# Causal attention: row maxima of two heads in one VectorE instruction over two PSUM banks

## The chip, the cores and the metric

The kernel runs on one core of one Trainium2 chip. The metric is the device time of one execution in microseconds (us). The engines named below are TensorE (PE, with its weight loads as PEld), VectorE (DVE), ScalarE (ACT), GpSimd (POOL) and SyncE (SP), which only issues DMAs. A PSUM bank holds 512 f32 numbers for each of 128 partitions.

## The reference, cut to what matters

The kernel computes one whole layer: a norm, a compressed, selected and windowed attention, a second norm, causal attention with 16 query and 4 key heads, and a mixture of 8 experts. The change touches the causal attention alone (here B = 2 batches, S = 2048 tokens, 16 numbers a head):

```python
q = _apply_rope(q, cos, sin)
k = _apply_rope(k, cos, sin)
scores = jnp.einsum('bqhd,bkhd->bhqk', q, k) * scale
causal = jnp.tril(jnp.ones((S, S), dtype=bool))
scores = jnp.where(causal[None, None], scores, jnp.finfo(scores.dtype).min)
probs = jax.nn.softmax(scores, axis=-1)
attn = jnp.einsum('bhqk,bkhd->bqhd', probs, v).reshape(B, S, NH * HD)
```

The softmax needs the largest score of each row before its exponentials can be taken.

## The kernel before, in words

`stage6` does this attention, about half of the span. Its work goes by 8 groups `gi` (2 batches x 4 key heads), each with `GRP` = 4 query heads, and in a group by 4 chunks `c` of 512 queries. Every score is computed twice.

**The main steps.** `STEPS` lists 320 steps (gi, c, kt), 40 in a group, where kt is a tile of 128 keys. For a step, TensorE multiplies keys by queries for 4 heads into `pS` (line 1558; I call one of these an S), with a second small matmul that adds the mask where the tile lies on the diagonal (line 1562). The matmul takes the row maximum with it, as three extra rows of `QT`. ScalarE takes the exponential into `prob` (line 1674, 3 slots of `pS`), and TensorE multiplies `prob` by the values into `pO` (line 1577: 4 heads, called PV). PV of step n - 1 stands in the middle of step n, and S of step n + 1 is issued in step n. When a chunk of queries is through, VectorE copies `pO` to `oS` (line 1747, `chunk`), and the first PV of the next chunk waits for that copy (`o_out`). TensorE then transposes `oS` into a bank of `pM` (line 1586, item O), and VectorE divides out of it (lines 1754 and 1756).

**The row maxima.** Ahead of that, a "unit" U (gi, head, query tile qt, part of 512 keys) computes the scores of 128 queries against up to 512 keys into one of `BANKS` = 4 banks of `pM` (line 1542), and VectorE takes the maximum of each row. Off the diagonal (part < qt // 4; 96 of the 160 units of a group) that is `reduce_max` over one full bank (line 1731). On the diagonal (64 units of 128 to 512 columns) it is an instruction that adds `mask_row` and takes the maximum (line 1727), with a short one that reads the result. After the last unit of a chunk one small VectorE instruction joins the parts (line 1739, `mneg`), POOL splits the result in three, and an item M transposes it into a bank (line 1533), from which ScalarE copies it to `mrow` and SP puts it into `QT`.

**What sets the order.** `background` lists units and M items; `schedule` gives every step its share of them by `cost`; in a step TensorE issues them at five places (`some(0)` to `some(4)`): ahead of the first S, after the first S, after the second S, after PV, and after the third S. `Plan` hands out the banks of `pM` in that order, one after the other, to U, M and O alike, and notes for each what must have left its bank before (`clear`). TensorE takes its instructions in order, so a unit that waits for its bank holds back the S and PV behind it. VectorE takes the units in the same order, and the copy of `pO` stands behind the units of its step. The units of chunks 0 and 1 of the first group, and some more, come ahead of the first step (`before`).

Of the kernel before, what the change touches and what calls it, by code (L numbers as in the profile page):

```python
# [30 lines left out]
P = 128  # L31
# [1126 lines left out]
def background():  # L1158

    items = []  # L1160
    for gi in range(NG):
        for c in range(CH):
            items += [("U", gi, h, qt, part) for h in range(GRP) for qt in range(4 * c, 4 * c + 4) for part in range(c + 1)]
            items.append(("M", CH * gi + c))

    for k in range(CH * NG - 1):
        at = items.index(("M", k))
        items.insert(at + 10, items.pop(at))
    return items
# [55 lines left out]
class Plan:  # L1225


    def __init__(self):
# [12 lines left out]
        for n, item in enumerate(order):  # L1241
            by = {"M": "mrow_out", "U": "unit_max", "O": "o_put"}[item[0]]
            counts[by] += 1
            self.bank[item], self.clear[item], self.count[item] = n % BANKS, last[n % BANKS], counts[by]
            last[n % BANKS] = (by, counts[by])
        self.units_through = {}
        for k in range(CH * NG):
            self.units_through[k] = max(self.count[x] for x in order if x[0] == "U" and CH * x[1] + x[3] // 4 == k)
        self.last_unit = {x: CH * x[1] + x[3] // 4 for x in order
                          if x[0] == "U" and self.count[x] == self.units_through[CH * x[1] + x[3] // 4]}  # L1250


def stage6(nc, sb, ps, sem, env, base_env):
# [7 lines left out]
    with ExitStack() as ctx:  # L1261
# [81 lines left out]
        with nc.Block() as block:  # L1343
# [150 lines left out]
            def _(pe):  # L1494
# [22 lines left out]
                    project(i)  # L1517

                def take(item):
                    if plan.clear[item] is not None:  # L1520
                        name, count = plan.clear[item]
                        pe.wait_ge(s[name], count)
                    return plan.bank[item]

                def beside(item):
# [162 lines left out]
            def _(dve):  # L1688
# [25 lines left out]
                assert first.k == 15  # L1714

                def beside(item):
                    if item[0] != "U":
# [4 lines left out]
                    if part == qt // 4:  # L1722
                        if plan.count[item] <= 2:
                            dve.wait_ge(s.masks, 1)
                        else:
                            dve.wait_ge(s.unit_max, plan.count[item] - 2)
                        nc.vector.tensor_tensor_reduce(junk[:, plan.count[item] % 2, 0:w], pM[:, plan.bank[item], 0:w],  # L1727
                                                       mask_row[:, 512 - w:512], 1.0, -3e38, ALU.add, ALU.max,
                                                       mx[:, h, qt, part:part + 1]).then_inc(s.unit_max, 1)
                    else:  # L1730
                        nc.vector.reduce_max(mx[:, h, qt, part:part + 1], pM[:, plan.bank[item], 0:w],  # L1731
                                             AX.X).then_inc(s.unit_max, 1)
# [816 lines left out]
```

## Time and profile before

| | |
|---|---|
| time, median of 3 runs | 1742.45 us (1739.26 to 1745.59) |
| span of the profiled execution | 1739.7 us |
| TensorE busy in it | 1630.1 us (94%) |
| VectorE busy | 1173.3 us (67%) |
| ScalarE busy | 946.3 us (54%) |
| granted TensorE clock, mean | 0.966 |
| the steps of the causal attention | about 352 to 1221 us |
| one group of 40 steps | 108.4 us |

The span is the time from the first to the last instruction of one profiled execution on the core; the profile has no other time of that execution, so the 2.75 us between the span and the median are taken as what lies around it. Busy time counts an instruction from its start to its end. Since the matmuls are pipelined, the busy time of TensorE contains the time in which a matmul drains while the next one already runs; the distance between two starts says more than the duration. A granted clock of 1.00 is 2.4 GHz and one of 0.50 is 1.2 GHz.

### The profile page before, as it was taken

The numbers are of one execution on the slowest core, as the hardware profiler recorded it, in microseconds if no ns is written. First come the engines' busy times: TensorE is split into PE (matmuls) and PEld (weight loads), VectorE is DVE, ScalarE is ACT, GpSimd is POOL, SyncE is SP. The second block draws the span as 40 slices with busy tenths as digits, with TensorE's granted clock in tenths as the row PEclk, the third lists the DMA queues.
The fourth block names the chain that finished last, engine by engine and source line by source line (L and its number), as shares of the span: only waits on it lengthen the run. The fifth ranks groups of instructions, "written<-read, shape, count | busy, mean of one in ns | idle before, by whom it ended". The sixth has DMA issues, their size and how long they took to land. (4 is left out here: it accounts for less than half of the span.)

```text
span 1739.7 us, 29572 instructions
## 1 busy us (share of the span) xinstructions
PE 1630.1 (94%) x9040; PEld 804.0 (46%) x9040; DVE 1173.3 (67%) x3195; ACT 946.3 (54%) x2069; POOL 556.3 (32%) x842
## 2 busy tenths in 40 slices
PE   7799998899999999999999999998895899999996
PEld 3367665333333333333333333332784455555564
DVE  6632788799888888888888888880685334434342
ACT  6034554256677676776767767677574233333332
POOL 3441238073515003030030300000277344444443
PEclk9899998799999999999999999999996899999999
DMA  5000000311030300303003030000378677777774
GB/s 164 0 7 19 1 2 7 61 26 38 1 62 2 59 4 1 62 2 59 5 1 62 2 61 3 2 1 1 99 238 286 117 130 129 130 129 129 132 125 71
DMA packets 252194, 105.76 MB, mean 61 GB/s; under 512 B 208064, under 2 KB 247880, under 8 KB 252040
## 3 DMA queue, kind: packets, MB, share of 16 engines
q1 hardware_dynamic: 233296, 80.62, 21.8%
q0 software_dynamic: 13392, 18.49, 6.3%
q10 hardware_dynamic: 5352, 4.76, 0.8%
q8 instruction: 76, 1.25, 0.3%
q14 instruction: 78, 0.64, 0.1%
HBM read 30.88 MB, written 23.67 MB: 31 GB/s over the span
## 5 line engine op out<-in xcount | busy, mean ns | idle before, releaser
L1674 ACT ACTIVATE prob<-pS 128x512 f32<-128x512 f32 (+3 forms) x1280 | 597.1, 534 | 256.3 <-PE pS L1562 134.1
L1731 DVE TENSOR_REDUCE mx<-pM 128x1 f32<-128x512 f32 x768 | 503.1, 686 | 70.3 <-PE pM L1542 66.5
L1542 PE MATMUL pM<-KT,QT 96*128 96x512 bf16 (+3 forms) x1280 | 444.1, 357 | 8.7 <-DMA QT<-Qt 4.6
L1558 PE MATMUL pS<-QT,KT 99*128 99x512 bf16 (+3 forms) x1280 | 416.5, 350 | 3.7 <-ACT prob L1674 2.8
L1577 PE MATMUL pO<-prob,VV 128*32 128x512 f32 (+3 forms) x2560 | 299.9, 540 | 14.6 <-ACT prob L1674 14.3
L2437 PE MATMUL bank<-w13T,QKV 128*128 x568 | 257.8, 598 | 16.5 <-ACT QKV L2464 16.5
L1727 DVE CUSTOM_DVE_ANT_0 junk<-pM,mask_row 128x128 bf16<-128x128 f32 (+3 forms) x512 | 241.6, 484 | 46.3 <-PE pM L1542 42.9
L1542 PEld LDWEIGHTS pM<-KT,QT 96*128 96x128 bf16 x1280 | 124.2, 98 | 268.5 <-DVE mx L1731 109.9
L1467 POOL CAST mpart<-mneg 128x16 bf16<-128x16 f32 x32 | 6.8, 211 | 663.2 <-DVE mneg L1739 663.2
L2497 DVE TENSOR_TENSOR QKV<-QKV,bank 128x512 f32<-128x512 f32 x71 | 48.9, 688 | 234.3 <-issue 199.1
L1558 PEld LDWEIGHTS pS<-QT,KT 99*128 99x128 bf16 x1280 | 123.6, 98 | 143.0 <-ACT prob L1674 79.8
L2418 POOL DMA_INDIRECT out_dram<-QKV x71 | 111.8, 1575 | 199.0 <-ACT QKV L2479 120.2
L2437 PEld LDWEIGHTS bank<-w13T,QKV 128*128 128x128 f32 x568 | 109.1, 192 | 124.6 <-issue 121.2
L2479 ACT ACTIVATE QKV<-bank,QKV 128x256 f32<-128x256 f32 x71 | 33.6, 474 | 206.9 <-DMA out_dram<-QKV 150.7
L2448 PE MATMUL bank<-w2T,QKV 128*128 x568 | 134.4, 380 | 2.4 <-DVE QKV L2511 2.4
L2448 PEld LDWEIGHTS bank<-w2T,QKV 128*128 128x128 f32 x568 | 108.0, 190 | 46.9 <-issue 36.0
L1562 PE MATMUL pS<-mask_kq,identb 128*128 128x128 bf16 x512 | 112.0, 221 | 0.0
L1577 PEld LDWEIGHTS pO<-prob,VV 128*32 128x32 f32 x2560 | 51.3, 108 | 114.2 <-ACT prob L1674 95.2
L2406 POOL COPY QKV<-QKV 128x512 uint16<-128x512 uint16 x71 | 81.8, 1152 | 18.0 <-issue 10.6
L1907 POOL DMA_INDIRECT queue<-QKV x64 | 65.2, 1019 | 20.9 <-issue 17.3
L1562 PEld LDWEIGHTS pS<-mask_kq,identb 128*128 128x128 bf16 x512 | 50.5, 99 | 37.3
L2464 ACT COPY QKV<-QKV 128x512 uint16<-128x512 uint16 x71 | 53.5, 754 | 20.5 <-DMA QKV<-QKV 18.5
(356 smaller groups left out, 1954.6 us busy)
## 6 DMA issues: line engine op xcount, KB each, us to landing
raw<-in_ffn_w_dram SPq DMA_DIRECT2D x48, 256.0 KB, 3.6
QKV<-queue SPq DMA_DIRECT2D x71, 136.0 KB, 2.6
out_dram<-x ACTq DMA_DIRECT2D x8, 512.0 KB, 4.7
x<-_attn_hidden_states_dram SPq DMA_DIRECT2D x14, 256.0 KB, 5.9
QKV<-QKV SPq DMA_TRANSPOSE x142, 3.3
QT<-mrow SPq DMA_DIRECT2D x128, 3.0 KB
out_dram<-QKV POOLq DMA_INDIRECT x71, 3.9
wc_s<-in_attn_Wc_dram SPq DMA_DIRECT2D x1, 1024.0 KB, 7.9
```

The costliest lines, as they stand in the source:

```text
L1542: last = nc.tensor.matmul(pM[:, bank, 0:w], QT[0:ROWS, par, h, qt * P:(qt + 1) * P], KT[0:ROWS, par, 512 * part:512 * part + w], start=Tru ...
L1558: last = nc.tensor.matmul(pS[:, p % NSC, lo:512], KT[0:ROWS + 3, par, kt * P:(kt + 1) * P], QT[0:ROWS + 3, par, h, 512 * c + lo:512 * c + ...
L1562: last = nc.tensor.matmul(pS[:, p % NSC, lo:lo + P], identb[:, :], mask_kq[:, :], start=False, stop=True)
L1577: last = nc.tensor.matmul(pO[32 * h:32 * h + 32, lo:512], VV[:, gi % 2, kt, :], prob[:, n % 3, h, lo:512], start=(kt == 0), stop=(kt == 4 ...
L1674: nc.scalar.activation(prob[:, n % 3, h, lo:512], pS[:, p % NSC, lo:512], ACT.Exp, scale=SCALE).then_inc(s.head_exp, 1)
L1727: nc.vector.tensor_tensor_reduce(junk[:, plan.count[item] % 2, 0:w], pM[:, plan.bank[item], 0:w], mask_row[:, 512 - w:512], 1.0, -3e38, AL ...
L1731: nc.vector.reduce_max(mx[:, h, qt, part:part + 1], pM[:, plan.bank[item], 0:w], AX.X).then_inc(s.unit_max, 1)
L1907: nc.gpsimd.indirect_dma_start(out=v.queue[:, :], out_offset=bass.IndirectOffsetOnAxis(ap=slots[:, t, a:a + 1], axis=0), in_=QKV[:, t, 0:R ...
L2406: nc.gpsimd.tensor_copy(xp[:, j % 2, :].rearrange("p (a n) -> p a n", a=2), apart(xq[:, j % R, 0:H], C)).then_inc(s.x_parts, 1)
L2418: nc.gpsimd.indirect_dma_start(out=v.out_rows[:, :], out_offset=bass.IndirectOffsetOnAxis(ap=tail[:, j % RT, E:E + 1], axis=0), in_=y[:, j ...
L2437: last = nc.tensor.matmul(pH[:, j % 2, a, :], xqT[:, j % 2, c * P:(c + 1) * P], w13T[:, c, bass.ds(e * (2 * FFN) + a * FFN, FFN)], start=( ...
L2448: last = nc.tensor.matmul(pY[:, j % 2, 0:H], gT[:, j % 2, f * P:(f + 1) * P], w2T[:, f, bass.ds(e * H, H)], start=(f == 0), stop=(f == FC ...
```

## The change

Off the diagonal, units of two neighbouring heads (2 pr and 2 pr + 1) with the same query tile and part become one item V. TensorE still does the two matmuls, one right after the other, now into two neighbouring banks (0 and 1, or 2 and 3), with one semaphore increment after the second. VectorE takes both rows of maxima with one `tensor_reduce` over 2 x 512 numbers. Diagonal units stay single. A V takes banks only from an even one on, so a bank is passed over where the count stands at an odd one. The order of the units is new (by pairs of heads instead of by head), M items are put 7 items later instead of 10, and `cost` gives a V 1134 where two units had 1244.

```diff
@@ background
-            items += [("U", gi, h, qt, part) for h in range(GRP) for qt in range(4 * c, 4 * c + 4) for part in range(c + 1)]
+            for pr in range(GRP // 2):
+                for qt in range(4 * c, 4 * c + 4):
+                    items += [("V", gi, pr, qt, part) for part in range(c)]
+                    items += [("U", gi, 2 * pr + n, qt, c) for n in range(2)]
...
-        items.insert(at + 10, items.pop(at))
+        items.insert(at + 7, items.pop(at))
@@ cost
+    if item[0] == "V":
+        return 2 * 512 + 110
@@ Plan
+            wide = 2 if item[0] == "V" else 1
+            if wide == 2 and free % 2:
+                free += 1
+            bank = free % BANKS
+            free += wide
...
+            before = [x for x in last[bank:bank + wide] if x]
+            self.clear[item] = [(name, max(k for n, k in before if n == name)) for name in sorted({n for n, _ in before})]
+            last[bank:bank + wide] = [(by, counts[by])] * wide
@@ stage6, TensorE
+                    if kind == "V":
+                        for n in range(2):
+                            last = nc.tensor.matmul(pM[:, bank + n, :], QT[0:ROWS, par, 2 * h + n, qt * P:(qt + 1) * P],
+                                                    KT[0:ROWS, par, 512 * part:512 * part + 512], start=True, stop=True)
+                        last.then_inc(s.unit_mm, 1)
+                        return
@@ stage6, VectorE
+                    if item[0] == "V":
+                        nc.vector.tensor_reduce(mx[:, 2 * h:2 * h + 2, qt, part],
+                                                pM[:, plan.bank[item]:plan.bank[item] + 2, :], AX.X,
+                                                ALU.max).then_inc(s.unit_max, 1)
+                        return
```

Over the kernel 768 single units become 384 V; 512 diagonal units, the matmuls and their sizes stay as they are.

**First place: the first step of chunk 1 in the second group.** TensorE, from one PV to the next, the last of chunk 0. In these rows `pM` is written by U and V, `pS` by S and by its mask, `pO` by PV. Before:

```order
L1577 MATMUL pO<-prob,VV 32x256 x4
L1558 MATMUL pS<-QT,KT 128x512
L1542 MATMUL pM<-KT,QT 128x512
L1558 MATMUL pS<-QT,KT 128x512
L1542 MATMUL pM<-KT,QT 128x512
L1558 MATMUL pS<-QT,KT 128x512
L1562 MATMUL pS<-mask_kq,identb 128x128
L1542 MATMUL pM<-KT,QT 128x512
L1558 MATMUL pS<-QT,KT 128x512
L1562 MATMUL pS<-mask_kq,identb 128x128
L1542 MATMUL pM<-KT,QT 128x256
L1577 MATMUL pO<-prob,VV 32x128 x4
```

After, the same stretch (line 1551 is a V, line 1559 a single unit, 1575 and 1579 the S and its mask, 1594 the PV):

```order
L1594 MATMUL pO<-prob,VV 32x256 x4
L1575 MATMUL pS<-QT,KT 128x512
L1551 MATMUL pM<-KT,QT 128x512 x2
L1575 MATMUL pS<-QT,KT 128x512 x2
L1579 MATMUL pS<-mask_kq,identb 128x128
L1551 MATMUL pM<-KT,QT 128x512 x2
L1575 MATMUL pS<-QT,KT 128x512
L1579 MATMUL pS<-mask_kq,identb 128x128
L1551 MATMUL pM<-KT,QT 128x512 x2
L1594 MATMUL pO<-prob,VV 32x128 x4
```

Where four single units stood, each with an S behind it, there are now six matmuls in three V with S between them, and three V need three pairs of banks where there are two.

VectorE ahead of the copy of `pO` (line 1747 before, 1765 after) that follows. Before:

```order
L1731 TENSOR_REDUCE mx<-pM 128x1 x3
L1727 ISA junk,mx<-pM,mask_row 128x256
L1727 ISA mx 128x1
L1731 TENSOR_REDUCE mx<-pM 128x1 x2
L1747 COPY oS<-pO 128x512
```

After:

```order
L1739 TENSOR_REDUCE mx<-pM 128x2 x3
L1748 ISA junk,mx<-pM,mask_row 128x128
L1748 ISA mx 128x1
L1748 ISA junk,mx<-pM,mask_row 128x128
L1748 ISA mx 128x1
L1765 COPY oS<-pO 128x512
```

The copy stood behind two reductions of one bank; it now stands behind two diagonal units and, ahead of these, three V, the second and third of which were issued before the PV.

**Second place: chunk 3 of the second group, from the PV of step 70 of the program to the PV of step 71.** TensorE before:

```order
L1577 MATMUL pO<-prob,VV 32x512 x4
L1542 MATMUL pM<-KT,QT 128x512
L1558 MATMUL pS<-QT,KT 128x512
L1533 MATMUL pM<-identb,mpart 12x128 x4
L1558 MATMUL pS<-QT,KT 128x512 x2
L1542 MATMUL pM<-KT,QT 128x512
L1558 MATMUL pS<-QT,KT 128x512
L1542 MATMUL pM<-KT,QT 128x512
L1577 MATMUL pO<-prob,VV 32x384 x4
```

TensorE after:

```order
L1594 MATMUL pO<-prob,VV 32x512 x4
L1559 MATMUL pM<-KT,QT 128x128
L1575 MATMUL pS<-QT,KT 128x512
L1551 MATMUL pM<-KT,QT 128x512 x2
L1575 MATMUL pS<-QT,KT 128x512 x2
L1551 MATMUL pM<-KT,QT 128x512 x2
L1575 MATMUL pS<-QT,KT 128x512
L1559 MATMUL pM<-KT,QT 128x256
L1594 MATMUL pO<-prob,VV 32x384 x4
```

Here a V into banks 0 and 1 is followed by a V into banks 2 and 3 and then by a unit of 256 columns into bank 0, with no PV between the first V and the unit.

## Rows read from the trace of the kernel before

**Rows 1.** By stretch: length; busy PE, PEld, DVE, ACT, POOL; clock, DMA share, GB/s.

```profile
335.00:340.00 5.00, 4.41 (x14) 1.27 (x14) 5.00 (x16) 0.57 (x1) 0.00 (x0) 0.50 0.01 2
...
500.00:600.00 100.00, 98.13 (x677) 36.78 (x677) 85.96 (x225) 70.32 (x150) 29.31 (x53) 1.00 0.06 13
```

**Rows 2.** The waits, 350 to 1150 us: who for whom, total, times, longest.

```profile
PEld pM L1542 <- DVE mx L1731: 96.1, 143, 0.8
...
PE pM L1542 <- DVE mx L1731: 0.2, 1, 0.2
```

**Rows 3.** Timeline, TensorE around one PV: start, duration, what, [idle before <-releaser].

```profile
672.35 0.33 PE L1542 MATMUL pM<-KT,QT 96*128 96x384 bf16 x1
672.60 1.06 PE L1577 MATMUL pO<-prob,VV 128*32 128x512 f32 x8
673.60 0.39 PE L1542 MATMUL pM<-KT,QT 96*128 96x512 bf16 x1
```

**Rows 4.** Timeline at the ends of three chunks (of chunk 0, 1 and 3).

```profile
591.96 0.68 DVE L1747 COPY oS<-pO 128x512 f32<-128x512 f32 x1
592.04 0.38 PE L1542 MATMUL pM<-KT,QT 96*128 96x512 bf16 x1
...
592.74 1.07 PE L1577 MATMUL pO<-prob,VV 128*32 128x512 f32 x8 [0.32 <-ACT prob L1674]
...
504.62 0.38 PE L1542 MATMUL pM<-KT,QT 96*128 96x512 bf16 x1
504.84 0.68 DVE L1747 COPY oS<-pO 128x512 f32<-128x512 f32 x1
...
505.63 1.07 PE L1577 MATMUL pO<-prob,VV 128*32 128x512 f32 x8 [0.63 <-ACT prob L1674]
...
581.51 0.22 PE L1562 MATMUL pS<-mask_kq,identb 128*128 128x128 bf16 x1
581.87 0.68 DVE L1747 COPY oS<-pO 128x512 f32<-128x512 f32 x1
...
582.65 1.07 PE L1577 MATMUL pO<-prob,VV 128*32 128x512 f32 x8 [0.92 <-ACT prob L1674]
```

**Rows 5.** VectorE's groups by shape, 350 to 1150 us: count | busy, mean ns.

```profile
L1731 DVE TENSOR_REDUCE mx<-pM 128x1 f32<-128x512 f32 x723 | 473.7, 686 | 67.7 <-PE pM L1542 64.2
...
L1727 DVE CUSTOM_DVE_ANT_0 junk<-pM,mask_row 128x512 bf16<-128x512 f32 x117 | 79.9, 683 | 5.6 <-PE pM L1542 5.6
...
L1727 DVE CUSTOM_DVE_ANT_0 junk<-pM,mask_row 128x128 bf16<-128x128 f32 x117 | 33.1, 283 | 3.7 <-PE pM L1542 3.7
```

**Rows 6.** Timeline: VectorE with work waiting (three reductions back to back).

```profile
706.05 1.88 DVE L1731 TENSOR_REDUCE mx<-pM 128x1 f32<-128x512 f32 x3
```

**Rows 7.** Timeline: from a unit's matmul to its reduction on an idle VectorE.

```profile
578.17 0.22 PE L1562 MATMUL pS<-mask_kq,identb 128*128 128x128 bf16 x1
...
578.23 0.38 PE L1542 MATMUL pM<-KT,QT 96*128 96x512 bf16 x1
...
578.43 0.60 ACT L1674 ACTIVATE prob<-pS 128x512 f32<-128x512 f32 x1 [0.51 <-PE pS L1562]
578.45 0.38 PE L1558 MATMUL pS<-QT,KT 99*128 99x512 bf16 x1
...
578.65 0.69 DVE L1731 TENSOR_REDUCE mx<-pM 128x1 f32<-128x512 f32 x1 [1.39 <-PE pM L1542]
```

**Rows 8.** Timeline: an S that comes too early for its slot of pS.

```profile
605.62 0.38 PE L1542 MATMUL pM<-KT,QT 96*128 96x512 bf16 x1
605.97 0.10 PEld L1558 LDWEIGHTS pS<-QT,KT 99*128 99x128 bf16 x1 [0.31 <-ACT prob L1674]
```

**Rows 9.** Timeline ahead of the first step, TensorE and VectorE.

```profile
339.31 1.00 PE L1542 MATMUL pM<-KT,QT 96*128 96x512 bf16 x2 [0.30 <-DVE mx L1731]
...
340.38 0.28 DVE L1727 CUSTOM_DVE_ANT_0 junk<-pM,mask_row 128x128 bf16<-128x128 f32 x1
340.59 0.08 DVE L1727 DVE_READ_ACCUMULATOR2_ANT mx<- 128x1 f32 x1
```

More of the change, by code:

```diff
@@ L1240, in __init__ @@
         last = [None] * BANKS
-        for n, item in enumerate(order):
-            by = {"M": "mrow_out", "U": "unit_max", "O": "o_put"}[item[0]]
-            counts[by] += 1
-            self.bank[item], self.clear[item], self.count[item] = n % BANKS, last[n % BANKS], counts[by]
-            last[n % BANKS] = (by, counts[by])
-        self.units_through = {}
+        free = 0
+        for item in order:
+            by = {"M": "mrow_out", "U": "unit_max", "V": "unit_max", "O": "o_put"}[item[0]]
+            wide = 2 if item[0] == "V" else 1
[3 more added lines that the diff above has]
+            free += wide
+            counts[by] += 1
+            self.bank[item], self.count[item] = bank, counts[by]
+            before = [x for x in last[bank:bank + wide] if x]
+            self.clear[item] = [(name, max(k for n, k in before if n == name)) for name in sorted({n for n, _ in before})]
+            last[bank:bank + wide] = [(by, counts[by])] * wide
+        self.last_unit = {}
         for k in range(CH * NG):
-            self.units_through[k] = max(self.count[x] for x in order if x[0] == "U" and CH * x[1] + x[3] // 4 == k)
-        self.last_unit = {x: CH * x[1] + x[3] // 4 for x in order
-                          if x[0] == "U" and self.count[x] == self.units_through[CH * x[1] + x[3] // 4]}
+            units_of = [x for x in order if x[0] in "UV" and CH * x[1] + x[3] // 4 == k]
+            self.last_unit[max(units_of, key=lambda x: self.count[x])] = k
 def stage6(nc, sb, ps, sem, env, base_env):
@@ L1519, in take @@
                 def take(item):
-                    if plan.clear[item] is not None:
-                        name, count = plan.clear[item]
+                    for name, count in plan.clear[item]:
                         pe.wait_ge(s[name], count)
@@ L1716, in beside @@
                 def beside(item):
-                    if item[0] != "U":
+                    if item[0] == "M":
                         return
@@ L1720, in beside @@
                     dve.wait_ge(s.unit_mm, plan.count[item])
-                    w = unit_width(qt, part)
[L1722 to L1729, printed above, removed]
-                    else:
-                        nc.vector.reduce_max(mx[:, h, qt, part:part + 1], pM[:, plan.bank[item], 0:w],
-                                             AX.X).then_inc(s.unit_max, 1)
+                    if item[0] == "V":
[3 more added lines that the diff above has]
+                        return
+                    w = unit_width(qt, part)
+                    if plan.count[item] <= 2:
+                        dve.wait_ge(s.masks, 1)
+                    else:
+                        dve.wait_ge(s.unit_max, plan.count[item] - 2)
+                    nc.vector.tensor_tensor_reduce(junk[:, plan.count[item] % 2, 0:w], pM[:, plan.bank[item], 0:w],
+                                                   mask_row[:, 512 - w:512], 1.0, -3e38, ALU.add, ALU.max,
+                                                   mx[:, h, qt, part:part + 1]).then_inc(s.unit_max, 1)
                     if item in plan.last_unit:
```

## The prediction

> **What bounds the kernel now.** I read the busy time by stretch first: in the causal attention, where the whole change lies, TensorE shows 98 us of 100 and VectorE 86, at a clock of 1.00; ahead of the first step it is the other way round, VectorE 5.00 us of 5.00, TensorE's clock 0.50 [rows 1].
>
> Next the waits. TensorE's weight loads seem to wait 96 us for VectorE's maxima, TensorE's matmuls 0.2 us [rows 2]. The timeline settles it. A PV starts 0.25 us after the matmul before it, whose 384 columns take 0.16 of that, and holds TensorE for 1.00 us; the load behind it stands idle until then whatever VectorE does [rows 3]. So those 96 us are mostly the PV itself, and no bank is waited for. I laid the instructions of one group one after the other: 0.22 us for 512 columns, in proportion for fewer, 0.06 for the mask matmul [rows 7], 1.00 for a full PV and 0.09 ahead of each [rows 3]. It comes to 104.5 us; the group takes 108.4. TensorE bounds the steps.
>
> Real waits stand where a chunk ends: PV waits for the copy of pO. Beyond the last matmul and the usual 0.09, it starts 0.39, 0.70 and 0.99 us late at three of the four ends (592.74 - 592.04 - 0.31; 505.63 - 504.62 - 0.31; 582.65 - 581.51 - 0.15) [rows 4]: 2.1 us a group. Some S come a little early for their slot (0.13 us at 605.97) [rows 8].
>
> **What VectorE saves.** A reduction of a bank takes 686 ns [rows 5], but three in a row take 1.88 us, so one occupies 0.60 [rows 6]. What a column costs the diagonal instruction shows: 683 ns for 512 and 283 for 128 [rows 5] are 400 ns for 384 columns, 0.53 us for 512. So 0.60 - 0.53 = 0.06 us of an instruction doesn't grow with its columns, and a V should take 0.69 + 0.53 = 1.22 us, 1.13 back to back. Bounds for a V: 1.07 (twice 0.53, nothing fixed) and 1.37 (two single ones, nothing saved). So 384 V save 384 x 0.064 = 25 us of VectorE, about 3 us of its time in a group. That lies beside TensorE's work and gives the span nothing directly; only the 2.1 us of copy waits a group and the stretch ahead of the first step could take from it. TensorE's matmuls stay: 104.4 us a group by the same sum.
>
> First the row, then the rule: with TensorE at its issue rate and VectorE at 86% [rows 1], VectorE isn't saturated in the steps. The Trainium skill (Perfetto Trace Analysis, "Optimizing Scalar/DVE Operations") puts about 125 ns on each VectorE instruction that touches PSUM and says grouping helps if the engine is saturated; that would be 384 x 0.125 = 48 us of VectorE. The same section says that where an engine isn't saturated but causes bubbles on others, breaking instructions up may help, which speaks against this change. The trace agrees with the condition, not yet with the bubble.
>
> **What TensorE pays.** A bank's turn, measured: the reduction starts 0.42 us after a 512-column matmul starts [rows 7], takes 0.69, and the waiting matmul starts 0.10 us after VectorE ends (591.96 + 0.68 to 592.74) [rows 4]: 1.2 us for a single bank. A V: second matmul 0.22 later, 1.22 of reduction: 0.22 + 0.42 + 1.22 + 0.10 = 1.95 us for two of the four banks. For every unit I took the natural time since its bank was last used and set it against this turn. Before, none of the 160 units falls short. After, 11 of the group's do, with VectorE idle otherwise. At the second place of the order, V, S, S, V, S, unit gives 0.43 + 0.22 + 0.22 + 0.43 + 0.22 = 1.52 us: the unit waits 0.43, with two more S and a PV queued behind it. This is so four times in a group; once it is 0.48, and three more are 0.09, 0.09 and 0.19. Together 2.6 us.
>
> **The chunk ends, worked out.** At the first place, with the first V at 0: the second V starts at 0.93, the third could at 1.63 but its banks are free at 1.95 (+0.32). VectorE runs the V from 0.63, 1.76 and 2.89. PV is at 2.47, the diagonal unit behind it waits for the second V until 3.08 (+0.25), the V in the next step 0.03. The third reduction ends at 4.11, two diagonal units take 0.20 each (a next one starts 0.21 after a first) [rows 9], the copy 0.68: PV starts at 5.20 instead of 4.73 (0.47, where it was 0.39). That end costs 0.7 us more. Chunk 1's end the same way: 0.85 against 0.70. Chunk 2's: 0.19 for a bank and 0.20 for the copy, against nothing. Chunk 3's: 0.97 against 0.99. Sum 1.2 us.
>
> **S in a row.** Two matmuls at one place leave others empty, so S follow each other sooner. A slot of pS turns in 0.20 + 0.22 + 0.60 + 0.07 us (the exponential starts 0.20 after the mask or the drain, takes 0.60 [rows 7], and frees it). By the same count S fall short by 0.6 us a group before (the 0.13 is one of them [rows 8]) and by 2.0 after; some of these stand behind a wait already counted, I take +1.0.
>
> Sum: 2.6 + 1.2 + 1.0 = 4.8 us a group. Steps 0 to 300 of 320 carry units, 7.5 groups: 36 us.
>
> **Ahead of the first step** VectorE is the bound for some 20 us at a clock of 0.50, where two matmuls take 1.00 us [rows 9]. The 12 V there save 12 x 0.06 = 0.8 us. But with V, unit, unit over four banks, the next V is filled only when the last has gone: 0.10 + 0.43 + 0.63 = 1.16 us (two matmuls at half clock and the drain), while VectorE has two diagonal units, 0.4 to 1.2 us by width. It idles about 0.75, 0.5, 0.2 and 0 us, twice: 2.9, and 1 us in the items of chunk 2. Net +3.
>
> The M items come about as many steps behind the last unit and ahead of their chunk as before (1.7 to 4 and 3.3 to 15 steps), so I cost them at nothing; a POOL chain of 1.7 us hides in the former. SP and POOL keep their order.
>
> The median is 2.75 us above the span; taken as unchanged. 1742.45 + 36 + 3 = **1781 us**.
>
> **The rivals.**
> - **Faster: VectorE's relief decides.** The copy waits go (2.1 x 8 = 17 us) and the stretch ahead gains 1: 1724 us. For it: VectorE stands between TensorE and PV there. Against: each of these copies is now behind V of 1.13 us that were issued late. It decides if the banks' turns are hidden, that is if a V's turn is below 1.5 us. Chance 0.07. If VectorE were the bound all along, the rule's first half, the 25 us of the rows would be the gain, 1717; I count it here.
> - **Same.** The waits for banks only take the place of waits for the copy, since a late PE finds the copy done: within 5 us. Chance 0.08.
> - **Slower, and no gain per V.** The reduction over two banks costs 1.37 us: 0.15 more at 11 banks and 3 copies, 2 us a group, 15 in all, 1796 us. In part the change then doesn't do what it says. Chance 0.08.
> - **The clock falls.** TensorE had 0.50 while it waited for VectorE again and again [rows 1, 9]; more waits in the steps could bring stretches of it. A tenth of the stage at half clock costs 80 us: 1860. The waits of up to 1 us at chunk ends left it at 1.00 [rows 1, 4]. Chance 0.02.
> - **The forecast**, 0.75: slower by the banks' turns. Its own range is 1760 to 1800: if waits early in a step absorb later ones half the sum is left (+20), and a backlog of VectorE that I left out adds 1 us a group, 8 us and more.
>
> **How the numbers follow.** The measurement tells about 0.3%, 5 us, from no change. Slower by more: 0.75 + 0.08 + 0.02 = 0.85; same 0.08; faster 0.07. The range takes in the forecast and the costly V and leaves out the faster rival, half of the same and the clock: 1754 to 1802.
>
> **What would show it.** One group takes 113 us instead of 108.4. A V's row reads 1.2 us. In the waits TensorE's matmuls into pM (not only the loads) wait for VectorE's maxima, some 2 to 4 us a group, none over 0.5 each. VectorE's busy share in the steps falls from 86 to about 80%. PV at chunk 0's end is 0.5 us late. I am wrong if the groups still take 108 us (then the turn is hidden), or if the time is lost in exponentials or in M items rather than at banks.

## The result, and the profile after

| | before | after |
|---|---|---|
| median | 1741.16 us of 4 runs (1739.26 to 1745.59) | 1789.97 us of 4 runs (1787.97 to 1790.42) |
| profiled execution: span | 1739.7 us | 1786.3 us |
| first S of the attention starts | 352.28 us | 355.27 us |
| one group (40 steps) | 108.41 us | 113.16 us |

The ratio is 1.0283, interval 1.0269 to 1.0296: the changed kernel is slower by 2.8%, 48.8 us, and 46.6 us by the spans of the two profiled executions. The forecast was 1781 us.

The page of the changed kernel, its head (engine, busy time, share of the span, instructions):

```profile
span 1786.3 us, 29219 instructions
...
PE 1644.7 (92%) x9040; PEld 799.6 (45%) x9040; DVE 1154.5 (65%) x2811; ACT 958.5 (54%) x2069; POOL 555.3 (31%) x842
```

The two stretches of [rows 1], now in the kernel after (length; busy PE, PEld, DVE, ACT, POOL; clock, DMA share, GB/s):

```profile
335.00:340.00 5.00, 4.11 (x12) 0.83 (x9) 4.37 (x9) 0.57 (x1) 0.00 (x0) 0.50 0.01 2
500.00:600.00 100.00, 96.91 (x650) 35.00 (x648) 79.47 (x172) 69.85 (x147) 28.22 (x48) 1.00 0.16 28
```

VectorE fell from 86 to 79.5 us in 100, as forecast, and the clock stayed at 1.00. About half of this fall is VectorE's saving: for one group its busy time is 93.2 us before (0.860 x 108.41) and 89.9 after (0.795 x 113.16), so 3.3 us less, and the rest is the longer group. TensorE's busy time fell by only 1.2 us, but its matmuls fell from 677 to 650, by 4%. The count is the better reading: a matmul's row is longer than the time that it holds the engine (0.38 us against 0.22), so the tail of each row covers part of the gap behind it. The group length says the same as the count, 113.16 / 108.41 = 1.044. One group is the distance between two copies of `pO` at the same place of the order. After, the timeline of VectorE:

```profile
611.04 0.68 DVE L1765 COPY oS<-pO 128x512 f32<-128x512 f32 x1
...
724.20 0.69 DVE L1765 COPY oS<-pO 128x512 f32<-128x512 f32 x1
```

The first of these before is in [rows 4], at 591.96; the second, of the kernel before:

```profile
700.37 0.68 DVE L1747 COPY oS<-pO 128x512 f32<-128x512 f32 x1
```

The new instruction in VectorE's groups by shape, 350 to 1200 us (count | busy, mean ns | idle before it <-releaser), to be set beside 686 ns for a single bank [rows 5]:

```profile
L1739 DVE TENSOR_REDUCE mx<-pM 128x2 f32<-128x1024 f32 x365 | 436.1, 1222 | 115.5 <-PE pM L1551 113.3
```

The waits in the same stretch (who for whom: total, times, longest). Where [rows 2] had 0.2 us, once, for TensorE's matmuls into `pM`, there are now 54 waits:

```profile
DVE mx L1739 <- PE pM L1551: 113.3, 167, 1.8
...
PE pM L1559 <- DVE mx L1739: 12.5, 46, 0.6
...
PE pM L1551 <- DVE mx L1739: 3.0, 8, 0.7
```

15.5 us over 7.5 groups is 2.1 us a group, at matmuls alone. The other side is as plain: VectorE stands idle 113 us ahead of its V, waiting for TensorE, where it was 66.5 us ahead of the single reductions in the same stretch before. Both engines wait for each other by turns, which neither did to this extent before.

**Where the 46.6 us lie.** I followed the 32 copies of `pO`. The fifth, early in the second group, comes at 483.55 us before and 497.88 after, so it is 14.3 us late; the 29th is 42.4 late, the last 45.7 (1220.69 and 1266.41). So: 3.0 us ahead of the first step, 11.3 from there to the fifth copy, 4.7 in each of the next six groups, 3.3 behind them, 0.9 after the attention. The stretch to the fifth copy is the first group and the first chunk of the second, 44 steps; below I call it the first group.

**Inside a group.** The first place of the order, the end of chunk 0, TensorE after:

```profile
606.55 0.60 PE L1551 MATMUL pM<-KT,QT 96*128 96x512 bf16 x2
...
607.48 0.59 PE L1551 MATMUL pM<-KT,QT 96*128 96x512 bf16 x2
...
608.48 0.60 PE L1551 MATMUL pM<-KT,QT 96*128 96x512 bf16 x2
609.01 0.43 PE L1594 MATMUL pO<-prob,VV 128*32 128x128 f32 x8
609.60 0.23 PE L1559 MATMUL pM<-KT,QT 96*128 96x128 bf16 x1 [0.17 <-DVE mx L1739]
...
610.79 0.10 PEld L1575 LDWEIGHTS pS<-QT,KT 99*128 99x128 bf16 x1 [0.47 <-ACT prob L1691]
...
611.02 0.60 PE L1551 MATMUL pM<-KT,QT 96*128 96x512 bf16 x2
611.83 1.06 PE L1594 MATMUL pO<-prob,VV 128*32 128x512 f32 x8 [0.20 <-ACT prob L1691]
```

And VectorE beside it:

```profile
607.19 3.49 DVE L1739 TENSOR_REDUCE mx<-pM 128x2 f32<-128x1024 f32 x3 [0.94 <-PE pM L1551]
```

With the first V at 0, the second is at 0.93 (predicted 0.93), the third at 1.93 (1.95), the diagonal unit at 3.05 (3.08), PV at 5.28 (5.20). The third V reuses the first one's banks, and its start is the turn of 1.95 us. The V ahead of PV is at 4.47 where the forecast's numbers give 4.20 (4.73 less 0.31 and 0.22), since the S ahead of it waited for its slot of `pS` (the load at 610.79); so the wait of PV for the copy is only 611.83 - 611.24 - 0.31 = 0.28 us where I had 0.47, and the end comes out at the same time.

The second place, TensorE after:

```profile
687.65 0.60 PE L1551 MATMUL pM<-KT,QT 96*128 96x512 bf16 x2
...
688.52 0.59 PE L1551 MATMUL pM<-KT,QT 96*128 96x512 bf16 x2
688.96 0.38 PE L1575 MATMUL pS<-QT,KT 99*128 99x512 bf16 x1
689.57 0.28 PE L1559 MATMUL pM<-KT,QT 96*128 96x256 bf16 x1 [0.24 <-DVE mx L1739]
```

and VectorE:

```profile
688.29 2.36 DVE L1739 TENSOR_REDUCE mx<-pM 128x2 f32<-128x1024 f32 x2 [0.35 <-PE pM L1551]
```

The unit needs a bank of the V at 687.65 and starts 1.92 us after it (0.06 us after VectorE is through with the first V of its row, at 688.29 + 1.22 = 689.51, where I had taken the 0.10 of a PV behind the copy); the S ahead of it ends its issue at 688.96 + 0.22 = 689.18, so 0.39 us are lost, against 0.43 predicted.

**The first group** is another matter. The stretch from the first S to the fifth copy, before:

```profile
352.30:483.50 131.20, 127.81 (x867) 48.61 (x867) 119.20 (x307) 88.40 (x190) 69.92 (x105) 0.99 0.11 22
```

and after:

```profile
355.30:497.80 142.50, 132.35 (x862) 48.34 (x861) 115.26 (x240) 89.97 (x190) 66.87 (x100) 0.97 0.10 20
```

It is nearly the same work, 862 and 867 matmuls recorded. TensorE is idle 10.15 us instead of 3.39, and the clock is 0.97 instead of 0.99. By these rounded shares the half-speed time costs some 4 us (0.03 x 142.5) where it cost 1.3. Six or seven of the 11.3 us are thus waits, some 3 the clock. This group's steps carry their own units and those of the next group, and they are dense. Twenty microseconds of it, before:

```profile
360.00:380.00 20.00, 18.85 (x133) 7.28 (x132) 19.71 (x50) 12.15 (x27) 12.32 (x20) 1.00 0.01 2
```

and after, with two short stretches at a lower clock behind it:

```profile
360.00:380.00 20.00, 17.16 (x123) 6.55 (x120) 17.85 (x34) 10.97 (x24) 11.54 (x13) 1.00 0.00 1
...
422.00:426.00 4.00, 3.29 (x18) 0.80 (x17) 3.63 (x9) 0.77 (x2) 0.39 (x2) 0.80 0.00 0
426.00:430.00 4.00, 4.00 (x27) 1.70 (x25) 2.39 (x11) 1.91 (x5) 3.68 (x9) 0.78 0.00 0
```

Before, VectorE was busy 19.71 of 20 us: here it set the pace, and here a saving of VectorE time might have paid. After, it is busy 17.85 and idle 2.15: the rows show it waiting for TensorE's V, whose two banks must both be filled first. Its timeline and TensorE's there:

```profile
368.27 2.36 DVE L1739 TENSOR_REDUCE mx<-pM 128x2 f32<-128x1024 f32 x2 [1.18 <-PE pM L1551]
```

```profile
360.82 0.34 PE L1559 MATMUL pM<-KT,QT 96*128 96x384 bf16 x1 [0.60 <-DVE mx L1739]
...
364.75 0.39 PE L1559 MATMUL pM<-KT,QT 96*128 96x512 bf16 x1 [0.32 <-DVE mx L1739]
```

### The profile page after: what moved, and what is told of

Read it like the earlier page. It is cut to its first block and busy times, and to the rows that moved or that the text cites. A ratio compares the mean times of both kernels' runs of the same rounds, so it can differ in the third digit from the quotient of the medians.

```text
span 1786.3 us, 29219 instructions
## 1 busy us (share of the span) xinstructions
PE 1644.7 (92%) x9040; PEld 799.6 (45%) x9040; DVE 1154.5 (65%) x2811; ACT 958.5 (54%) x2069; POOL 555.3 (31%) x842
## 5 line engine op out<-in xcount | busy, mean ns | idle before, releaser
L1691 ACT ACTIVATE prob<-pS 128x512 f32<-128x512 f32 (+3 forms) x1280 | 607.7, 533 | 281.6 <-PE pS L1579 145.3
L1739 DVE TENSOR_REDUCE mx<-pM 128x2 f32<-128x1024 f32 x384 | 459.1, 1222 | 121.2 <-PE pM L1551 118.9
L1575 PE MATMUL pS<-QT,KT 99*128 99x512 bf16 (+3 forms) x1280 | 398.4, 351 | 8.7 <-ACT prob L1691 5.2
L1748 DVE CUSTOM_DVE_ANT_0 junk<-pM,mask_row 128x128 bf16<-128x128 f32 (+3 forms) x512 | 235.4, 486 | 58.4 <-PE pM L1559 54.6
L1551 PE MATMUL pM<-KT,QT 96*128 96x512 bf16 x768 | 234.3, 387 | 11.4 <-DVE mx L1739 8.8
L2515 DVE TENSOR_TENSOR QKV<-QKV,bank 128x512 f32<-128x512 f32 x71 | 48.8, 688 | 236.1 <-issue 206.1
L1559 PE MATMUL pM<-KT,QT 96*128 96x128 bf16 (+3 forms) x512 | 153.5, 310 | 22.4 <-DVE mx L1739 13.0
L1559 PEld LDWEIGHTS pM<-KT,QT 96*128 96x128 bf16 x512 | 49.6, 98 | 162.2 <-DVE mx L1739 72.8
L1551 PEld LDWEIGHTS pM<-KT,QT 96*128 96x128 bf16 x768 | 63.2, 98 | 102.1 <-DVE mx L1739 36.1
```

Source lines behind the costliest of these rows:

```text
L1551: last = nc.tensor.matmul(pM[:, bank + n, :], QT[0:ROWS, par, 2 * h + n, qt * P:(qt + 1) * P], KT[0:ROWS, par, 512 * part:512 * part + 512 ...
L1559: last = nc.tensor.matmul(pM[:, bank, 0:w], QT[0:ROWS, par, h, qt * P:(qt + 1) * P], KT[0:ROWS, par, 512 * part:512 * part + w], start=Tru ...
L1575: last = nc.tensor.matmul(pS[:, p % NSC, lo:512], KT[0:ROWS + 3, par, kt * P:(kt + 1) * P], QT[0:ROWS + 3, par, h, 512 * c + lo:512 * c + ...
L1691: nc.scalar.activation(prob[:, n % 3, h, lo:512], pS[:, p % NSC, lo:512], ACT.Exp, scale=SCALE).then_inc(s.head_exp, 1)
L1739: nc.vector.tensor_reduce(mx[:, 2 * h:2 * h + 2, qt, part], pM[:, plan.bank[item]:plan.bank[item] + 2, :], AX.X, ALU.max).then_inc(s.unit_ ...
```

## The experiments

The theory: a V fills, holds and frees two banks at once, and the time is lost at the banks' turns. The rivals: the place and price that the planner gives to V and M items, the new order of the units, the instruction itself, or the copy behind the V. The times stand beside those of the kernel before on the same chip; each has the median, the ratio with its interval, the shift of the first S and of the fifth copy against before, and the length of a later group.

**Each bank by itself.** Plan, order and places of the changed kernel stay; the hand-over is per bank.

```diff
@@ TensorE, V
+                            if n and plan.second[item]:
+                                pe.wait_ge(s[plan.second[item][0]], plan.second[item][1])
...
-                        last.then_inc(s.unit_mm, 1)
+                            last.then_inc(s.unit_mm, 1)
@@ VectorE, V
-                        nc.vector.tensor_reduce(mx[:, 2 * h:2 * h + 2, qt, part], ...
+                        for n in range(2):
+                            dve.wait_ge(s.unit_mm, plan.count[item] - 1 + n)
+                            nc.vector.reduce_max(mx[:, 2 * h + n, qt, part:part + 1], pM[:, plan.bank[item] + n, :],
+                                                 AX.X).then_inc(s.unit_max, 1)
```

> The changed kernel with its order, its places and its even banks, but the two banks of a V are handed over one by one: each matmul signals by itself, VectorE takes a maximum over one bank at a time, and each bank is free after its own. Theory (the turn of a bank pair, 1.95 us, holds TensorE): the waits at the banks go, what stays is the order with two matmuls at one place, +1 us a group by the count of early S: a group takes 109 to 110 us, the kernel 1745 to 1762 us. Rival (the new order, the M items and the clumps of matmuls cost the time): it stays within 10 us of the changed kernel's 1790 us and a group at 112 to 113 us.

Measured: 1764.64 us, 1.0133 (1.0116 to 1.0151); first S -0.5, fifth copy +4.4, group 110.33 us. The total is 2.6 us above the range, the group 0.33 above its own. Its copies of `pO`, a group apart:

```profile
598.29 0.69 DVE L1770 COPY oS<-pO 128x512 f32<-128x512 f32 x1
...
708.61 0.68 DVE L1770 COPY oS<-pO 128x512 f32<-128x512 f32 x1
```

The hand-over by pairs is 113.16 - 110.33 = 2.83 us of a group, and 9.9 of the 14.3 us up to the fifth copy: 25 us of the 49. Some 1.9 us a group stay with the placement; the table behind the last experiment says where. One piece of them can be seen at the first place, TensorE of this kernel:

```profile
593.84 0.60 PE L1555 MATMUL pM<-KT,QT 96*128 96x512 bf16 x2
...
597.78 0.60 PE L1555 MATMUL pM<-KT,QT 96*128 96x512 bf16 x2
599.08 1.06 PE L1598 MATMUL pO<-prob,VV 128*32 128x512 f32 x8 [0.70 <-ACT prob L1695]
```

PV comes 5.24 us after the first pair, as it does in the changed kernel (5.28). At this place separate banks help nothing: three pairs of long reductions stand ahead of the copy, VectorE works them off back to back, and PV waits 599.08 - 598.00 - 0.31 = 0.77 us for the copy. What TensorE saves at the banks it loses again at the copy.

**Two instructions, handed over as a pair.**

```diff
-                        nc.vector.tensor_reduce(mx[:, 2 * h:2 * h + 2, qt, part], ...).then_inc(s.unit_max, 1)
+                        for n in range(2):
+                            last = nc.vector.reduce_max(mx[:, 2 * h + n, qt, part:part + 1], pM[:, plan.bank[item] + n, :], AX.X)
+                        last.then_inc(s.unit_max, 1)
```

> The changed kernel, but a V is taken by two one-bank maxima, and both banks are still filled and freed together. Theory: the turn grows from 1.95 to 2.0 us and VectorE's time by 0.06 a V: 0.06 at some 12 places, 0.7 us a group, and 3 in the first group: 1795 to 1802 us. Rival 1 (an instruction over two banks is slow in itself): faster than the changed kernel by more than 5 us. Rival 2 (VectorE's load bounds the steps): 25 us slower, 1815.

Measured: 1798.5 us, 1.0328 (1.031 to 1.0346); first S +2.9, fifth copy +16.3, group 114.12 us. VectorE's group by shape:

```profile
L1740 DVE TENSOR_REDUCE mx<-pM 128x1 f32<-128x512 f32 x722 | 453.3, 683 | 105.8 <-PE pM L1551 103.1
```

The merged instruction saves something once a pair is handed over as one: 8.5 us, about 1 us a group. It is the pair's hand-over that costs, not the instruction. The total is as expected, and both rivals are out.

**Half the columns read.** This kernel leaves out half of the keys off the diagonal from the maxima.

```diff
-                                         scale=SCALE).then_inc(s.head_exp, 1)
+                                         scale=SCALE / 16).then_inc(s.head_exp, 1)
...
-                                                pM[:, plan.bank[item]:plan.bank[item] + 2, :], AX.X,
+                                                pM[:, plan.bank[item]:plan.bank[item] + 2, 0:256], AX.X,
```

> The changed kernel, but the maximum over two banks reads only the first 256 columns of each, so the maxima leave out half the keys off the diagonal, and the exponentials get a sixteenth of the scale so that they stay finite; the shapes of ScalarE's and TensorE's work are unchanged. A V should take 0.69 us, its turn 1.42 us, below the 1.52 us between a V and the reuse of its bank. Theory: waits at banks in the steps go and the first group is no longer held: a group at 106 to 109 us, the kernel 1725 to 1752 us. Rival (it is not VectorE's time but that two banks must be free at once, or the order): stays above 1770 us.

Measured: 1741.2 us, 0.9994 (0.9981 to 1.0007); first S -2.4, fifth copy -4.5, group 108.2 us.

```profile
L1739 DVE TENSOR_REDUCE mx<-pM 128x2 f32<-128x512 f32 x372 | 256.5, 692 | 190.4 <-PE pM L1551 186.9
```

With 0.53 us less in the turn of two banks (1.42 instead of 1.95 us) the same plan, order and pairs take no more time than the kernel before. This takes time from the turn and load from VectorE together, so it doesn't tell these two apart. Nor does it show that the placement is free: by the table behind the last experiment the waits of S for a slot of `pS` stay as they are in the changed kernel, 2.3 us a group against 0.5 before, and are made up for by shorter waits for the copy, 0.7 against 2.1, since the reductions ahead of the copy are shorter. One of these S in this kernel, 0.45 us late:

```profile
664.90 0.39 PE L1575 MATMUL pS<-QT,KT 99*128 99x512 bf16 x1 [0.29 <-ACT prob L1691]
```

The run also shows that a turn below 1.5 us, the point at which I let the faster rival decide, would have brought the time back to that of before and not below it.

**The pairs from the second group on, and in the first group alone.** The first of these edits; the other has the condition turned round.

```diff
+            if gi == 0:
+                items += [("U", gi, h, qt, part) for h in range(GRP) for qt in range(4 * c, 4 * c + 4) for part in range(c + 1)]
+                items.append(("M", CH * gi + c))
+                continue
...
-        items.insert(at + 7, items.pop(at))
+        items.insert(at + (10 if k < 3 else 7), items.pop(at))
```

> The changed kernel with the units of the first of the 8 groups single, by head, as before; V from the second group on. It tells where the time lies: in the changed kernel the copy of pO at the end of the first group (fifth copy) comes 14.3 us later than before, of which 3.0 us lie ahead of the first step. Theory (the first group is filled so densely that VectorE is busy 19.7 of 20 us there, and every wait of a pair costs): that part goes and leaves 4.75 us a group for 6.6 groups, 31 us over before: 1770 to 1778 us. Rival (the late start moves the rest, or the clock's later rise carries on): below 1765 or above 1782.

Measured: 1773.73 us, 1.0176 (1.0157 to 1.0195); first S -0.4, fifth copy +2.0, group 113.15 us. It is as expected.

> V in the first group alone, the units of the other seven single and by head as before. Theory (the first group's loss is its own and what is ahead of the first step 3 us of it): the first copies come late as in the changed kernel, 14 us in all, and the later groups take 108.41 us again: 1752 to 1758 us. Together with V from the second group on (33 us slower) it should give the 48 us of the whole change. Rival (the late start is caught up, since the first group's units were only moved forward): below 1748 us.

Measured: 1751.21 us, 1.0059 (1.0042 to 1.0075); first S +0.7, fifth copy +6.4, and 108.41 us a group from there on. It missed: 6.4 of the 14.3 us by which the fifth copy is late. The later groups' share stands by itself (32.2 us). The first group alone costs 10.6 us and both together 42.7, not 48.8. In the whole change the units of group 1, done beside the steps of group 0, are pairs too; the two parts share those steps, and about 6 us arise only where both are there. They arise ahead of the fifth copy: +2.0 and +6.4 make 8.4 of the 14.3.

**The order alone.** The kernel before, its single units in the order of the pairs:

```diff
-            items += [("U", gi, h, qt, part) for h in range(GRP) for qt in range(4 * c, 4 * c + 4) for part in range(c + 1)]
+            for pr in range(GRP // 2):
+                for qt in range(4 * c, 4 * c + 4):
+                    items += [("U", gi, 2 * pr + n, qt, part) for part in range(c + 1) for n in range(2)]
```

> The kernel before with the new order of the units (by pairs of heads) and nothing else: single units, single banks, the same cost and the same M items as before. It splits the 1.92 us a group that the kernel with single handover still lost (110.33 us a group against 108.41). Theory (two matmuls at one place, which leave S matmuls in a row): counted like the prediction's, early S cost 0.7 us a group in this order and 0.6 before, so a group takes 108.4 to 108.8 us, the kernel 1740 to 1747 us. Rival (the order by pairs of heads costs it, at the chunk ends): 110 us a group, 1755 to 1765 us.

Measured: 1744.35 us, 1.002 (1.0011 to 1.003); first S +0.7, fifth copy +1.6, group 108.23 us. The order costs about 4 us (1.9 to 5.2 by the interval), and nothing in a group.

**Only the pairs that I named.** In the changed kernel ten V of the 48 of a group are handed over bank by bank: those whose banks my count found asked for before their 1.95 us are over.

```diff
+SPLIT = {(0, 12, 0), (0, 12, 1), (0, 13, 1), (0, 15, 1), (1, 13, 1), (1, 15, 2), (0, 5, 0), (0, 8, 0), (0, 9, 0), (1, 8, 0)}
```

> The changed kernel, but the 10 V of a group whose banks by the prediction's count are asked for before their 1.95 us are over (two of them share a waiting unit) are taken by two one-bank maxima with each bank freed by itself; the other 38 stay merged. Theory (the waits at just those places are the merging's whole price in the steps): a group takes 110.3 to 110.9 us, near the 110.33 of single handover for all; the first group, whose steps are filled differently, keeps part of its loss: 1768 to 1778 us. Rival (the price is spread, VectorE's backlog behind every V): 112 to 113 us a group, 1783 to 1790 us.

Measured: 1768.68 us, 1.0154 (1.0138 to 1.0171); first S +2.1, fifth copy +9.6, group 110.59 us. Ten V give back 2.57 of the 2.83 us that all 48 give. The places of my count are the right ones in a steady group, and handing over the other 38 as pairs costs 0.26 us there.

**The placement's price.** The kernel with separate banks once more, each V priced like two units (1244 instead of 1134) and M items put 8 items later instead of 7.

```diff
-        return 2 * 512 + 110
+        return 2 * (512 + 110)
...
-        items.insert(at + 7, items.pop(at))
+        items.insert(at + 8, items.pop(at))
```

> The kernel with the changed order and single handover, but a V counts in the planner what two units counted (1244 instead of 1134) and M items stand 8 items later. It splits the 2.1 us a group between it (110.33) and the single units in the same order (108.23). Theory (two matmuls at one place of a step, which leave other places empty): it stays at 109.8 to 110.8 us a group, 1758 to 1770 us. Rival (the planner's shares by the new cost): 109 us or less, below 1752 us.

Measured: 1775.71 us, 1.0199 (1.0182 to 1.0216); first S +2.4, fifth copy +5.5, group 112.45 us. Both theories missed, with the sign wrong: the old price and the later M items together make a group 2.1 us longer than the new price does. TensorE's waits for banks grow from 0.3 to 2.2 us a group although each bank is handed over by itself, those of S for a slot of `pS` from 2.2 to 2.6, and those for the copy shrink from 2.7 to 2.5. A change of a tenth in the price moves items across steps, and where they cluster is worth 2 us a group. The run changes two things at once, so it doesn't say which of them did it.

**The copy put ahead.** At a chunk's first step VectorE takes the copy of `pO` ahead of the units of the last two places (of five), instead of behind them all. On the kernel before:

```diff
-                    for x in plan.beside[n]:
+                    extra = plan.beside[n]
+                    at = 3 * len(extra) // 5 if n and kt == 0 else len(extra)
+                    for x in extra[:at]:
                         beside(x)
-                    for k in contexts(n):
-                        chunk_put(k)
                     if n and kt == 0:
                         chunk(CH * gi + c - 1, n)
+                    for x in extra[at:]:
+                        beside(x)
+                    for k in contexts(n):
+                        chunk_put(k)
```

> The kernel before, with the copy of pO moved in VectorE's queue: at the step in which a chunk ends it stands behind the units of the first three places, which TensorE issues before the last PV, and ahead of those of the last two. Theory (PV waits at chunk ends only because the copy stands behind units issued later): the 0.39, 0.70 and 0.99 us a group shrink to 0.1 or less each: a group at 106.5 to 107.2 us, the kernel 1725 to 1735 us. Rival (the late units then hold banks and move the wait there, or PV itself ends late): a group within 0.3 us of 108.41, 1739 to 1744 us.

Measured: **1727.26 us, 0.9918 (0.9893 to 0.9943)**; first S -1.6, fifth copy -2.8, group 106.34 us. It is faster than both kernels. The 100 us of [rows 1] in it:

```profile
500.00:600.00 100.00, 100.00 (x695) 37.74 (x697) 88.34 (x232) 71.75 (x155) 29.38 (x53) 1.00 0.09 17
```

A chunk's end in it, VectorE and then TensorE:

```profile
501.71 0.68 DVE L1747 COPY oS<-pO 128x512 f32<-128x512 f32 x1
```

```profile
502.68 0.38 PE L1542 MATMUL pM<-KT,QT 96*128 96x512 bf16 x1
502.99 1.07 PE L1577 MATMUL pO<-prob,VV 128*32 128x512 f32 x8
```

PV starts 0.31 us after the last matmul, 0.22 of issue and the usual 0.09: the wait of 0.70 us at this end [rows 4] is gone. A group gains 2.07 us, and the three waits in [rows 4] made 2.1. The total is as expected, the group a little below its range.

The same edit on the changed kernel:

> The same move of the copy in the changed kernel. Theory: the copy waits at the ends (0.5 to 0.9 us each by the prediction) go, but a pair behind the copy is freed 0.6 us later and some of it comes back: a group at 111.3 to 112.3 us, the kernel 1773 to 1783 us, still well above before. Rival (the chunk ends carry most of the change's loss): a group at 109 us or less, below 1765 us.

Measured: 1776.05 us, 1.0208 (1.019 to 1.0225); first S +2.9, fifth copy +10.5, group 111.67 us. The edit takes 1.5 us from a group of the changed kernel and 13.9 us from the whole, as against 2.07 and 12.8 us on the kernel before. So the changed kernel with the early copy is 48.8 us slower than the kernel before with the early copy (1776.05 and 1727.26), just what it is without (48.8): the waits for the copy, there in both, are next to no part of what the change costs.

**TensorE's gaps in a steady group.** From the ninth to the thirteenth copy I took the distance between every two starts on TensorE and subtracted what the first one needs (0.22 us for 512 columns and in proportion, 1.00 for a full PV and in proportion) and 0.09 ahead of a PV. What is left is a gap. Those over 0.04 us are put down to a bank where a VectorE row ended 0.06 us before the start of a unit or M item, to a slot of `pS` where an exponential ended 0.05 to 0.06 us before the start of an S, and to the copy where a PV of a chunk's end is late. In us a group:

| kernel | banks | slots of `pS` | copy | other gaps | group |
|---|---|---|---|---|---|
| before | 0 | 0.5 | 2.1 | 5.1 | 108.41 |
| changed | 3.5 | 2.3 | 2.3 | 4.4 | 113.16 |
| each bank by itself | 0.3 | 2.2 | 2.7 | 4.5 | 110.33 |
| two instructions, one hand-over | 4.3 | 2.3 | 2.5 | 4.4 | 114.12 |
| half the columns read | 0.1 | 2.3 | 0.7 | 4.5 | 108.20 |
| the order alone | 0 | 0.6 | 1.8 | 5.0 | 108.23 |
| ten V bank by bank | 0.5 | 2.3 | 2.6 | 4.5 | 110.59 |
| each bank by itself, old price | 2.2 | 2.6 | 2.5 | 4.5 | 112.45 |
| before, early copy | 0.1 | 0.5 | 0 | 5.0 | 106.33 |
| changed, early copy | 4.1 | 2.3 | 0 | 4.6 | 111.67 |

Without its gaps a group is 100.75 us in eight of them (before the table's rounding), so nothing else differs. In the two others (old price; changed, early copy) records of M items lie between those of a PV, and their other gaps are what is missing to the same 100.75. The table shows what stays with separate banks, 1.9 us a group: 1.7 more before S, 0.6 more at the copy, 0.3 at banks, and 0.7 less in the other gaps. S waits 2.2 to 2.6 us for its slots in all seven kernels with pairs in this group, and 0.5 or 0.6 in the three without: putting two matmuls at one place costs this, and the order of the units alone does not.

## Why the forecast was right, and where its sizes were off

**What bounds the steps: right.** TensorE sets the pace of a steady group; 3.3 us of VectorE time freed in a group brought it nothing. The rule that speaks against the change was borne out as well: the Trainium skill (Perfetto Trace Analysis, "Optimizing Scalar/DVE Operations") says that where an engine isn't saturated but makes others wait, breaking its instructions up may help, and here the same plan with the pairs broken up and handed over bank by bank is 25 us faster. It is the hand-over that does it: broken up but still handed over as a pair, it is 8.5 us slower. The Trainium skill's 125 ns for an instruction, from the same section, was 0.06 to 0.07 us in these runs (a V 1.22 us, two single ones back to back 1.29). The kernel with half the columns read shows the pace from the other side: VectorE at 63% (62.96 us in the 100 from 500 on) and a group of 108.2.

**The V's duration: right.** 1222 ns measured, 1.22 us worked out, so the third rival (1.37 us) is out. The timeline's three in a row, 3.49 us, are 1.22 + 2 x 1.13, as worked out.

**The turn: right.** 1.95 us worked out, 1.93 and 1.92 in the rows above, and the ten V that I counted carry 2.57 us of a group's 2.83. Before, my count found no unit of a steady group waiting and the table has none; after, it found 11 and the table's 3.5 us are 11 waits.

**A group: 4.8 predicted, 4.75 measured, but the parts differ.** By the table the waits for banks rose by 3.5 us (predicted 2.6 and about 0.8 within the chunk ends), those for slots of `pS` by 1.8 (my count gave 0.6 and 2.0, I took 1.0 of the 1.4), those for the copy by 0.2 (0.4), and the other gaps shrank by 0.7, for which the forecast has no term. I took off too much for S that stand behind a wait already counted, and that the sum is within 0.1 us is luck: the slots too small by 0.8 and the missing term cancel.

**Ahead of the first step: right in sum, +3 against +2.99.** With separate banks under the same plan it is -0.5, so the hand-over by pairs was the cause, about 3.5 us. The kernel with separate banks and the old price has +2.4 again; its plan puts one diagonal unit more ahead of the first step, and where the rest comes from is not shown.

**The term that was too small is "7.5 groups: 36 us".** I multiplied the steady group's loss by all groups. The 44 steps up to the fifth copy lost 11.3 us, where 4.8 us a group make 5.3. These steps carry units of two groups (by the plan 187 matmuls of units beside the first 40 steps, 160 beside those of each of the next five groups), and VectorE was busy there 19.71 of 20 us, which I hadn't looked at: my two windows were 335 to 340 and 500 to 600. By the count of the table TensorE waits for banks about 2.6 us between the first and the fifth copy already before, 8.8 after, and 5.5 with separate banks; "no bank is waited for" was true of the steady groups alone. Separate banks bring the fifth copy from +14.3 to +4.4. The clock is part of it too: half clock lasted until about 359.5 us, over 4 us into the steps, where it had lasted until 354.3, 2.0 us into them, and it fell again at 422 to 430 (rows in the last section). That was my last rival, "the clock falls", at 2%, which I had made to decide all or nothing; it was there on a scale of 3 us. With 11.3 in place of 5.3 the sum would have been 1787.5. Of the 9.8 us by which the change cost more than forecast (48.8 and 39), 6.0 lie here, 0.7 in the rest of the attention, 0.9 behind it, and 2.2 between the spans and the medians.

**The rivals.** "Faster" fails: no span of the steps gained from VectorE's relief. "Same" fails: the waits at the banks don't take the copy's place, which grew from 2.1 to 2.3 us a group, and with the copy put ahead in both kernels the difference is 48.8 us all the same. What I listed as a sign held but for two details: waits of TensorE's matmuls of 2.1 us a group (2 to 4), but the longest 0.7 us and not under 0.5; and PV at chunk 0's end late by 0.28 rather than 0.5.

**What stays open.** Why about 6 us arise only with pairs in both the first group and the later ones. Why TensorE waits 2.2 us a group for banks under the old price, although each bank is handed over by itself, and 0.3 under the new one. And what brought the clock down at 422 to 430 us.

## What to carry to other kernels

Merging two buffers' reads into one instruction saves one instruction's fixed part (0.06 us here) and doubles the unit that two engines hand to each other: set the turn of the merged buffer (1.95 us against 1.2) against the distance of its reuse in each place, and do it first in the densest stretch rather than in a typical one. Two matmuls at one place also let those of the main chain follow each other sooner, and these then wait for their own buffers: 1.7 us a group here, with separate banks too. Saved time on an engine is worth something only where that engine is waited for; a change of a few lines that put the awaited copy ahead of two fifths of its step's reductions gave 0.8%, while taking 19 us off VectorE's busy time (1173.3 to 1154.5) cost 2.8%.

## What the runs showed of the hardware

- A `tensor_reduce` over 2 x 512 f32 of two banks takes 1222 ns and one over 2 x 256 takes 692, against 683 to 686 for 512 of one bank. The time goes by the number of columns, and the step from bank to bank costs 6 to 9 ns at most.
- A unit's matmul that waits for its bank starts 0.06 us after VectorE's reduction ends (689.57 and 689.51 at the second place), an S that waits for its slot 0.05 to 0.06 us after ScalarE's, a PV that waits for the copy 0.10 us after VectorE's [rows 4].
- TensorE's clock gave way in the dense first group, which I had expected at 1.00. In the changed kernel TensorE's first steps ran at half speed for over 2 us longer: the mean clock from 355 to 360 us is 0.55, so 4.5 of these 5 us at 1.2 GHz; before, it is 0.77 from 352 to 357, so 2.3 us. At 422 to 430 us it was 0.80 and 0.78 after TensorE had stood idle 0.45 of 2 us (420 to 422) and while it stood idle 0.71 of 4; before, 410 to 440 us show 1.00. The rows of before:

```profile
352.00:357.00 5.00, 4.99 (x28) 2.31 (x26) 3.58 (x9) 4.19 (x9) 4.33 (x7) 0.77 0.01 2
...
420.00:440.00 20.00, 20.00 (x141) 7.33 (x140) 17.81 (x56) 15.04 (x32) 8.64 (x17) 1.00 0.01 2
```

The changed kernel:

```profile
355.00:360.00 5.00, 5.00 (x22) 2.38 (x20) 1.73 (x6) 3.64 (x7) 4.60 (x5) 0.55 0.01 2
...
420.00:422.00 2.00, 1.55 (x7) 0.50 (x6) 1.56 (x4) 1.36 (x3) 0.00 (x0) 1.00 0.00 0
...
420.00:440.00 20.00, 18.70 (x119) 6.63 (x117) 15.21 (x49) 11.85 (x27) 10.18 (x23) 0.91 0.00 1
```

The changed kernel with the early copy, where TensorE stands idle as much there (1.41 of 20 us against 1.30) and the clock stays at 1.00:

```profile
420.00:440.00 20.00, 18.59 (x133) 6.46 (x130) 17.03 (x53) 13.74 (x30) 12.28 (x25) 1.00 0.01 2
```

So the link between these waits and the clock is not shown; there is one trace of each kernel.
